# The routing exponentials of two expert layers by tanh and three small VectorE steps

## The reference, cut to what matters

```python
logits = x @ router_w + router_b            # 16 experts
topv, topi = jax.lax.top_k(logits, 4)
topw = jax.nn.softmax(topv, axis=-1)        # the exponentials
one_hot = (topi[..., None] == jnp.arange(E)).astype(topw.dtype)
scores = jnp.einsum('tk,tke->te', topw, one_hot)
gu = jnp.einsum('th,ehf->tef', x, gate_up_proj) + gate_up_bias
gate, up = jnp.minimum(gu[..., ::2], 7), jnp.clip(gu[..., 1::2], -7, 7)
act = (up + 1.0) * gate * jax.nn.sigmoid(gate * 1.702)
expert_out = jnp.einsum('tei,eih->teh', act, down_proj) + down_bias
out = jnp.einsum('te,teh->th', scores, expert_out)
```

## Time and profile before

| what | value |
|---|---|
| median of three runs | 802.87 us |
| profiled execution, its own time | 801.57 us |
| its span, first to last instruction | 799.8 us |
| mean granted TensorE clock | 0.931 of full speed |
| PE busy | 688.7 us, 86% |
| ACT busy | 570.4 us, 71% |
| DVE busy | 490.8 us, 61% |
| POOL busy | 270.9 us, 34% |

### The profile page before, as it was taken

The page is one execution under the profiler, slowest core; times in us unless marked ns, Lnnn a source line. Parts: engine busy times, 40 slices in busy tenths (PEclk is TensorE's granted clock), DMA queues, the critical chain, the costliest instruction groups (busy, mean ns, idle before and its releaser), DMA issues.

```text
span 799.8 us, 11151 instructions
## 1 busy us (share of the span) xinstructions
PE 688.7 (86%) x3617; PEld 406.2 (51%) x3617; DVE 490.8 (61%) x1259; ACT 570.4 (71%) x804; POOL 270.9 (34%) x298
## 2 busy tenths in 40 slices
PE   2789788888898899899877759999999999999587
PEld 2567566666566667677655532332323323332465
DVE  4789978879798888889856542344322222232474
ACT  4657575666767676565453659999999999999143
POOL 3286456755666555455520430022000000000110
PEclk9999999999999999899958688999999999999757
DMA  9001232323223223233200189000199100000001
GB/s 261 7 1 67 76 99 82 93 78 92 78 89 97 83 97 113 80 117 111 67 26 0 29 177 198 19 2 1 16 189 195 24 1 1 1 1 1 2 1 52
DMA packets 31341, 54.52 MB, mean 68 GB/s; under 512 B 4624, under 2 KB 13280, under 8 KB 29776
## 3 DMA queue, kind: packets, MB, share of 16 engines
q1 hardware_dynamic: 30128, 53.38, 25.1%
q0 software_dynamic: 224, 0.34, 0.2%
q10 hardware_dynamic: 928, 0.06, 0.1%
HBM read 35.71 MB, written 1.28 MB: 46 GB/s over the span
## 4 chain that ended last, share of the span: by engine, by line
ACT 28%; PE 17%; issue 8%; DVE 4%; POOL 3%; ACTq 0%; POOLq 0%; DVEq 0%
ACT raw_w L830 25%; PE bank L1393 3%; PE bank L1395 3%; PE bank L1394 3%; POOL act_parts L570 1%; PE bank L1690 1%; PE bank L1433 1%; ACT xt L659 1%; PE bank L1518 1%; PE bank L1515 1%; PE bank L1448 1%; PE bank L1516 1%; PE bank L1449 1%; PE bank L1674 1%; DVE xn_parts L934 1%
## 5 line engine op out<-in xcount | busy, mean ns | idle before, releaser
L830 ACT ACTIVATE raw_w<-bank,minus_c 128x1024 f32<-128x1024 f32 x256 | 259.4, 1156 | 5.2 <-DVE bank L1266 3.1
L570 POOL TENSOR_TENSOR act_parts<-act,act_parts 128x512 fp32r<-128x512 f32 x128 | 167.6, 1311 | 149.2 <-ACT act_parts L731 146.7
L1266 DVE TENSOR_TENSOR bank<-bank,fix 128x256 f32<-128x256 f32 x128 | 55.3, 432 | 180.7 <-PE bank L1674 180.7
L717 ACT ACTIVATE bank<-bank,b_gate 128x512 f32<-128x512 f32 x112 | 74.1, 661 | 86.4 <-PE bank L1395 86.3
L1393 PE MATMUL bank<-xn_parts,w_hi 128*128 128x512 f32 x256 | 110.2, 430 | 21.2 <-DVE up L1058 11.6
L1395 PE MATMUL bank<-xn_parts,w_hi 128*128 128x512 f32 x256 | 103.9, 406 | 0.0
L1394 PE MATMUL bank<-xn_parts,w_lo 128*128 128x512 f32 x256 | 103.6, 405 | 0.0
L1058 DVE TENSOR_SCALAR up<-bank,b_up 128x512 f32<-128x512 f32 x113 | 84.1, 744 | 21.6 <-PE bank L1395 20.6
L731 ACT ACTIVATE act_parts<-act 128x512 fp32r<-128x512 f32 x128 | 80.4, 628 | 23.4 <-DVE act L1076 22.0
L1076 DVE SCALAR_TENSOR_TENSOR act<-up,bank 128x512 f32<-128x512 f32 x128 | 88.0, 687 | 4.4
L514 POOL TENSOR_SCALAR var_eps<-mean_var 128x4 f32<-128x4 f32 x28 | 7.1, 254 | 238.0 <-DVE mean_var L928 236.6
(11 more groups left out here) (207 smaller groups left out, 1084.1 us busy)
## 6 DMA issues: line engine op xcount, KB each, us to landing
grow<-scores SPq DMA_DIRECT2D x68, 256.0 KB, 3.1
early<-scores SPq DMA_DIRECT2D x44, 256.0 KB, 3.2
raw_w<-in_gate_up SPq DMA_DIRECT2D x4, 512.0 KB, 8.9
w_lo<-gelu_parts SPq DMA_DIRECT2D x8, 256.0 KB, 5.1
w_lo<-act_parts SPq DMA_DIRECT2D x8, 256.0 KB, 5.5
w_hi<-gelu_parts SPq DMA_DIRECT2D x6, 256.0 KB, 4.6
w_hi<-act_parts SPq DMA_DIRECT2D x6, 256.0 KB, 5.6
x_tok<-in_x SPq DMA_DIRECT2D x4, 256.0 KB, 4.0
```

The source lines that it names most:

```text
L570: pool.tensor_tensor(act_lo[:, j % NACT, :], act[:, j % NACT, :], act_hi[:, j % NACT, :].bitcast(F32), ALU.subtract).then_inc(s["lo_ready" ...
L717: eng.activation(out, bank[:, G, :], ACT.Gelu_apprx_sigmoid, bias=b_gate[:, e:e + 1]).then_inc(s["glu_ready"], 1)
L830: eng.activation(probs[:, u % NP, :], pair, ACT.Exp, bias=minus_c[:, b:b + 1])\
```

## The change

For r < 2 the activation becomes tanh(-x/2), and three DVE steps turn it in place into exp(x)/2: add 1, take the reciprocal, which is (1 + exp(x))/2, and subtract a half. The factor of a half cancels when the picked values are divided by their sum. Each of the three steps waits for the one before on `pick_step`, whose counts grow from three to six for each such routing. The low-rank routers keep exp.

```diff
-                ne = E0 if r < 2 else E1
-                eng.activation(expd[:, kr % 2, :, 0:ne], shifted[:, kr % 2, :, 0:ne], ACT.Exp)\
-                   .then_inc(s["exp_ready"], 1)
+                if r < 2:
+                    eng.activation(expd[:, kr % 2, :, 0:E0], shifted[:, kr % 2, :, 0:E0], ACT.Tanh, scale=-0.5)\
+                       .then_inc(s["exp_ready"], 1)
+                else:
+                    eng.activation(expd[:, kr % 2, :, 0:E1], shifted[:, kr % 2, :, 0:E1], ACT.Exp)\
+                       .then_inc(s["exp_ready"], 1)
...
-                step = 3 * min(kr, 2 * NC) + 4 * max(kr - 2 * NC, 0)
+                step = 6 * min(kr, 2 * NC) + 4 * max(kr - 2 * NC, 0)
                 eng.wait_ge(s["exp_ready"], kr + 1)
                 eng.wait_ge(s["taken_step"], kr + 1)
+                if moe:
+
+                    half_exp = expd[:, b, :, 0:E0]
+                    eng.tensor_scalar(half_exp, half_exp, 1.0, None, ALU.add).then_inc(s["pick_step"], 1)
+                    eng.wait_ge(s["pick_step"], step + 1)
+                    eng.reciprocal(half_exp, half_exp).then_inc(s["pick_step"], 1)
+                    eng.wait_ge(s["pick_step"], step + 2)
+                    eng.tensor_scalar(half_exp, half_exp, -0.5, None, ALU.add).then_inc(s["pick_step"], 1)
+                    step += 3
+                    eng.wait_ge(s["pick_step"], step)
...
-                eng.wait_ge(s["pick_step"], 3 * min(kr + 1, 2 * NC) + 4 * max(kr + 1 - 2 * NC, 0))
+                eng.wait_ge(s["pick_step"], 6 * min(kr + 1, 2 * NC) + 4 * max(kr + 1 - 2 * NC, 0))
```

## The result

The changed kernel takes 811.01 us (median of four runs, 809.20 to 812.88) against 801.80 us before (four runs, 798.79 to 803.10): ratio 1.0116, 95% interval 1.0092 to 1.0141. It is slower, by 9.3 us. The forecast had the sign but 2.8 us for the size, and the measured time lies 1.5 us above the range.

The account below looks back on a forecast made before the run. PE and DVE share the bound, ACT has room. Terms 0.98 x 3 - 0.01 - 0.27 + 0.65 - 0.55 = +2.76 us give 804.3 on the profiled execution, 805.6 on the median; range 799.5 to 809.5.

Parts of the forecast that it names:

- job 11: Routing at job 11: PE already waits for the DVE chain, so the longer chain goes straight to PE, +0.98 us.
- job 18: Routing at job 18: DVE's wait for the gated function goes, -0.99, the longer chain adds +0.98; sum -0.01 us.
- job 53: Routing at job 53: PE's 0.28 us wait for ACT goes and DVE's slack covers nearly all the chain, -0.27 us.
- job 67: Routing at job 67: DVE's idle hides 0.29 of the added 0.98 us, and POOL's norm steps come later; +0.65 us.
- job 83: Routing at job 83: DVE's idle covers the chain and the gate bank is free 0.64 us earlier; -0.55 us.
- job 99: Routing at job 99: DVE's 2.86 us idle hides the chain and nobody waits for ACT; 0.
- faster: Rival, chance 0.20: at six load pairs the gain is 1.59 us each, 7.6 us faster in all, 795.3 us.
- drain: ACT's table loads: the Trainium skill gives about 1380 ns of drain beside each; the prediction's rows showed none at job 11.
- Size of the steps: Three DVE instructions per routing: 0.18, 0.51 and 0.18 us plus 0.10 between them, 0.98 us; bounds 0.6 and 1.1.
- The start: First two routings, before the jobs: no load goes, PE's transposes wait for the DVE chain, +0.98 us twice.
- the clock: Rival on PE's clock: a low stretch costs about half its length; given no sign, it only widens the range.
- blocked steps: Rival, chance 0.13: POOL holds the loop's twelve new tensor_scalars, 0.18 us each on average; +5.0 us in all, 807.9 us.

Follow-up runs that it names:

- e3: The changed kernel with the first two routings, before the jobs, back to exp without the three steps; ratio to the kernel before 1.0077.
- e6: The changed kernel with POOL's addition x<-tmp,x one job later in POOL's order; ratio to the kernel before 1.0078.
- e7: The changed kernel with the steps of the second pass's routings two jobs later on VectorE; 816.32 us, ratio to the kernel before 1.0178.
- e4: The changed kernel with only the routing at job 11 back to exp with its two table loads; ratio to the kernel before 1.0068.
- e5: The changed kernel with nine extra matmuls on PE at job 11 ahead of its wait for the shares; ratio to the kernel before 1.0127.
- e1: The changed kernel without the three added VectorE steps, weights computed from the tanh itself; 800.39 us, ratio to the kernel before 0.9977.
- e2: The changed kernel with exp and its table loads back but the three steps kept; 811.12 us, ratio to the kernel before 1.0109.
- e10: The kernel before with POOL's addition x<-tmp,x one job later and nothing else; ratio to the kernel before 1.0016.
- e9: The changed kernel with tanh and steps only at jobs 18 and 83, exp elsewhere, POOL's addition one job later; ratio to the kernel before 1.0005.
- e8: The changed kernel with exp in the first three routings and the other five's steps two jobs later; 807.21 us, ratio to the kernel before 1.0068.

## Why the prediction was wrong

Where other traces have the same instructions at a routing as the kernel after, the growth of the lag there can be compared, in us:

| routing | jobs | forecast | after | the same instructions |
|---|---|---|---|---|
| job 11 | 10 to 14 | +0.98 | +3.7 | e3 +3.7, e6 +3.7, e7 +4.2 |
| job 18 | 17 to 20 | -0.01 | -0.3 | e3 -0.4, e4 -0.3, e5 -0.3, e6 -0.4, e7 -0.3 |
| job 53 | 52 to 55 | -0.27 | +0.95 | e3 -0.1, e4 -0.1, e5 +0.9 |
| job 67 | 66 to 71 | +0.65 | +3.0 | e3 +1.7, e4 +1.7, e5 +1.8 |
| job 83 | 82 to 87 | -0.55 | 0.0 | e3 0.0, e4 -0.1, e5 0.0 |
| job 99 | 98 to 101 | 0 | -1.5 | e3 -1.5, e4 0.0, e5 +0.1 |

**What bounds the kernel, and the loads.** Right in the sum. ACT was the engine with room, and taking 15 us off it gave about 1.8 us (e1, interval 0 to 3.7); the waits of ACT that the prediction read come to about 1.9. The rival "faster" is refuted. The places agree less: e1's trace wins 2.2 us at job 18 where 0.99 was read, and loses 2.1 at job 67. No drain behind a load shows up either: in the trace after ACT's next instruction starts 0.01 us behind nine of the eleven loads.

**Size of the steps.** Nearly right: 1.05 us and not 0.98. The tensor_scalars take 0.19 and 0.20 us; the reciprocal takes 0.554, at the upper of my two slopes and not in the middle.

**The start: +1.96 forecast, +2.1 measured**; e3 takes it away. PE's two waits became

```profile
23.18 1.05 PE L1476 MATMUL bank<-ident,share_hl 128*48 128x128 f32 x4 [4.90 <-DVE share_hl L1030]
32.71 1.05 PE L1476 MATMUL bank<-ident,share_hl 128*48 128x128 f32 x4 [2.69 <-DVE share_hl L1030]
```

each 1.05 us longer than in the earlier trace rows. This is the firmest part of the 2.1; the lag itself is +0.8 to +3.2 at job 10 in the traces with the same start.

**Job 11: +0.98 forecast, +3.7 measured.** This is the step that failed. The prediction said "the longer chain goes straight to PE: +0.98". It does, but two things ride on it. Against before the chain from its first instruction to the last grew from 1.74 to 3.94 us, 1.05 by the steps and the other 1.15 by instructions that POOL held: line 998 and the first of line 1024 for 1.56 us after, line 983 for 0.40 before. And PE's wait of 2.79 us instead of 0.45 was followed by a low stretch of the clock, worth 1.5 us (e5, and e5 against e7). 1.05 + 1.15 + 1.5 = 3.7. Of this term of the sum, then, the steps were right, and the held instructions and the clock were put at nothing.

**Job 18: -0.01 forecast, -0.3 measured.** Right in kind, since DVE no longer waits for ACT there, but the terms that cancel were both half of what they are: the loads alone win 2.2 us here (e1) and the steps alone cost 2.0 (e2), against 0.99 and 0.98 forecast. That they cancel in the forecast as well is luck.

**Job 53: -0.27 forecast, +0.95 measured.** In e3 and e4, with the same instructions there, the routing costs nothing (-0.1 both), and in e2, with the loads, 0.0. After has a low stretch at 195.8 us and e5, which loses 0.9, has one at 197.9; e2, e3 and e4 have none. So the forecast is nearly right without the clock, and what the clock adds (1.1 us) comes in some traces only. It was not tested by itself.

**Job 67: +0.65 forecast, +3.0 measured.** By e6 the term without blocking or clock is 1.3. Of these 0.3 come from POOL's later addition itself, as e10 has them without any step; that leaves 1.0, the whole chain, so DVE's 0.29 us of idle hid nothing. Of the other 1.7 us the held step is 0.4 and the low stretch 1.3 (e3, e4, e5 against e6 and after). The prediction had both as things apart: the blocked steps as a rival at the average of 0.18 us a step, and the clock as something without a sign.

**Job 83: -0.55 forecast, 0.0 measured.** The first step was held here too (0.89 us), and ate the gain; with it free, e6 and e9 win 0.7. **Job 99: 0 forecast, -1.5 measured**, all clock, and no work of the change. The kernel before has 6.8 us of low clock there. Every trace that has as much stands at -0.2 to +0.1 (e2, e4, e5, e8, e9). With 3.4 us it is -1.5 (after, e3, e7, and e10, which has all loads and no steps). With none it is -2.9 and -3.0 (e6, e1).

**The rivals.** "Blocked steps" was the nearest, at +5.0; what it lacked is that it isn't alone. At job 11 the low clock is set off by the longer chain: it came in all five traces with the long wait of PE (2.7 to 3.8 us), in none with a shorter one (0.45 to 0.47, and 1.13 in e1), and not where the wait was filled. I priced POOL's holding only for the new steps, while the old ones of the chain, which read two SBUF tensors, were held as long (line 998 for 1.1 us). The trace before had shown that already, at job 18, where the prediction read only the wait for ACT:

```profile
89.81 1.31 DVE L1009 SCALAR_TENSOR_TENSOR share_hl<-picked,recip 128x64 f32<-128x64 f32 x2
```

"I give this no sign" was the mistake on the clock at job 11. For the loop as a whole the traces don't settle a sign: from the clock's first rise up to 390 us they have 24 us of low clock before and 27 after, 17 in e1 and 31 in e2, but 20 in e6 and e7, which have the steps.

## What to carry to other kernels

A table load on an engine with room is worth only the waits that others have for that engine at those places: read them one by one, and test by leaving out the replacement. Steps added to an engine that shares the bound cost their length where TensorE waits for it, and on top what TensorE's clock can lose behind a longer wait; here eight chains, each 1.05 us longer, cost 8.7 us (e2). When VectorE's small steps run beside a busy GpSimd, count every instruction of the chain as one that can be held, not only the new ones. And before a place in one trace is given a cause, look at the same place in a second trace with the same instructions: here job 67 lost 3.0 us in one and 1.7 in three others.

## What was unexpected of the hardware

A reciprocal of 64 elements per partition takes 0.554 us, against 0.178 for 4: 6.3 ns for each further element, while tensor_scalar on the same 64 takes 0.19. VectorE's held instructions of the chain end 0.05 to 0.09 us behind the end of GpSimd's running one, whether they read one SBUF tensor (0.87 us instead of 0.19) or two (1.28 instead of 0.22). Nine extra matmuls in a wait of TensorE kept its clock at 2.4 GHz (granted clock 1.00); without them it fell to 1.2 GHz behind the wait (0.66 over 5 us). A low stretch of 3.4 us cost 1.5 us at job 99, in a loop where TensorE is busy 89% of the time.
